# Spreading expert gates over the partitions by DMA instead of by a selection matmul, in an audio tower on one core

## Chip, cores and metric

One core of a Trainium2 chip. The metric is the device time of one execution in microseconds (us), lower is better. The kernel before was run three times, median 1820.26 us (1820.25 to 1823.58).

## What is computed

The reference is an audio tower of two layers over 4 sequences of 750 frames with 128 channels. Layer 0 is a dynamic convolution (31 taps), a dense convolution to 512 channels with SELU, a projection to 128 and a causal attention; its output has 720 positions per sequence, 2880 tokens in all. Layer 1 is an attention over 7200 keys per sequence and then a mixture of experts, which is what the change touches:

```python
router_probs = softmax(x @ router_w.T + bias)            # 64 experts
topk_p, topk_i = top_k(router_probs, 6); topk_p /= sum(topk_p) + 1e-9
# an assignment past the capacity C of its expert is dropped
hg = einsum('ecd,efd->ecf', expert_in, w_gate)           # F = 64
hu = einsum('ecd,efd->ecf', expert_in, w_up)
expert_out = einsum('ecf,edf->ecd', silu(hg) * hu, w_down)
out = x + shared_out + segment_sum(gate * expert_out)    # + 2 shared experts, halved
```

## The kernel before

The kernel (`tower`) has one instruction stream for each engine, and they wait for each other on semaphores. Stage 0 is layer 0, stage 1 the attention over the keys, stage 2 the experts. At the end of stage 1 all five engines meet at a barrier (`stage_end`).

**Router.** After the attention of sequence b its tokens go through the steps of `POST_STEPS`, which are laid by hand beside the tiles of the next sequence's attention (for the last sequence, beside the expert pairs of chunk 0, by the last number of each entry). The last steps are `gates`: VectorE multiplies probabilities and slots into `gate2` (L1219, twice, since the 64 experts stand in it twice), TensorE transposes it (L1512) to experts on 128 partitions, ScalarE writes the high halves as fp16 into `gates` and `g_tmp` (L804, L805), and VectorE writes the remainders into partitions 64 to 127 (L1226). So `gates` [128, 2880] holds the high fp16 part of a gate on partition e and the low part on partition 64 + e.

**Experts.** All experts are computed for all tokens. The tokens are cut into `NMC` = 6 chunks of `MT` = 480, and a chunk has `NSEQ` = 33 turns: turn 0 is the pair of shared experts, turns 1 to 32 (`PAIRS`) are pairs of routed experts, whose 2 x 64 hidden channels fill the 128 partitions. Inputs and weights are split in a high and a low fp16 part, so each product takes three matmuls. For turn n:

- TensorE, `up` (L1669): waits `up_free`, then 3 matmuls for the gate projection and 3 for the up projection (L1676 to L1678, once for each), and for a routed pair one more (L1682) with the 0/1 matrix `sel_sb`, which adds high and low part and spreads the two gates of the pair over 64 partitions each, into a third PSUM bank. That matmul signals `up_ps`.
- ScalarE, `silu` (L843): reads the gate projection.
- VectorE, `product` (L1278): L1282 multiplies silu (SBUF) with the up projection (PSUM) into `su`; L1288 multiplies `su` (SBUF) with the spread gates (PSUM) into `ac`, then `up_free` is raised. `shared_product` (L1296) has no gate.
- ScalarE, `high_part` (L849): fp16 copy `a_hi` of `ac`. In its order of work it stands behind the silu of turn n + 1.
- GpSimd, `low_part` (L643): `a_lo` = `ac` - `a_hi`, all three in SBUF.
- TensorE, `down` (L1686): 3 matmuls (L1690 to L1692) that add to the chunk's output.

Everything of a turn has two buffers. TensorE's order is up(n + 2), down(n), up(n + 3), down(n + 1), and so on. At the end of a chunk `chunk_done` copies the sum (L853), transposes it (L1699), adds the residual (L1305) and stores it from SyncE's queue (L538). Chunks 1 to 5 run in a hardware loop, chunk 0 is unrolled because of the router steps beside it. SyncE does nothing else in stage 2. In stage 1 it loads keys, values, `sel_sb` (L529) and the expert weights (L533).

Of the kernel before, what the change touches and what calls it, by code (L numbers as in the profile page):

```python
# [17 lines left out]
F32 = mybir.dt.float32  # L18
F16 = mybir.dt.float16
# [9 lines left out]
P = 120  # L29
# [89 lines left out]
def shared_turns():  # L119
# [4 lines left out]
    for b in range(B + 1):  # L124
        for x in steps + [(DOWN, B - 1, "h", k) for k in range(2)] * (b == B):
# [4 lines left out]
            if kind == MIX and at == 0:  # L130
# [30 lines left out]
              ("act", "gates", 0, 52, 26), ("dve", "gates", 1, 53, 27), ("pe", "gates", 1, 55, 28),  # L161
              ("act", "gates", 1, 56, 30), ("dve", "gates", 2, 56, 31)]
# [74 lines left out]
def tower(nc, d, out):  # L237
    ctx = ExitStack()
    with ctx:
# [54 lines left out]
        for n in range(2):  # L294
# [7 lines left out]
        sel_sb = region_k.take(PAIRS * 128, dtype=F16)  # L302
# [79 lines left out]
        gate2 = region_c.take(R, 2 * E)[0:P]  # L382
        g_tmp = region_c.take(T, dtype=F16)
# [13 lines left out]
        fin = region_c.take(MT // P, C)[0:P]  # L397

        band_dram = nc.dram_tensor("band_dram", [WT, NW, HEADS * WIN], F32).ap()
# [10 lines left out]
            shifted_logits logits_exp msk_ready gates_ready gates_hi  # L410
# [9 lines left out]
        s_tail = sem("tail_in")  # L420

# [59 lines left out]
        def _(sp):  # L481
# [47 lines left out]
            sp.dma_start(sel_sb, d["sel"]).then_inc(s["const_in"], 16)  # L529
# [6 lines left out]
            with sp.Fori(0, NMC) as c:  # L536
                sp.wait_ge(s["fin_ready"], c + 1)
                sp.dma_start(out_t[:, bass.ds(c * (MT // P), MT // P), :], fin).then_inc(s["fin_out"], 16)  # L538
# [119 lines left out]
        def _(act):  # L658
# [131 lines left out]
            def post(b, what, k):  # L790
# [11 lines left out]
                elif what == "gates":  # L802
                    act.wait_ge(s["post_full"], USE[POST, b, what, k])
                    a.activation(gates[0:E, b * T + k * HALF:b * T + (k + 1) * HALF], bank(bk, E)[:, 0:HALF], ACT.Copy)  # L804
                    a.activation(g_tmp[E:128, half], ps[E:128, bk, 0:HALF], ACT.Copy).then_inc(s["gates_hi"], 1)  # L805
# [72 lines left out]
        def _(dve):  # L878
# [263 lines left out]
            def post(b, what, k):  # L1142
# [74 lines left out]
                elif (what, k) == ("gates", 0):  # L1217
                    for n in range(2):
                        last = v.tensor_tensor(gate2[:, :, n * E:(n + 1) * E], slot[:, :, 0:E], probs[:, :, 0:E],  # L1219
                                               ALU.mult)  # L1220
                    own.link(last)
                    dve.sem_inc(s["gates_ready"], 1)
                elif what == "gates":
                    half = slice((k - 1) * HALF, k * HALF)
                    dve.wait_ge(s["gates_hi"], 2 * b + k)
                    own.link(v.tensor_tensor(gates[E:128, b * T + (k - 1) * HALF:b * T + k * HALF],  # L1226
# [99 lines left out]
        def _(pe):  # L1326
# [379 lines left out]
            for n in range(NSEQ):  # L1706
                if n + 2 < NSEQ:
                    up(0, n + 2, n + 1, n % 2, n + 2)
# [111 lines left out]
```

## Time and profile before

| | |
|---|---|
| median of three runs | 1820.26 us (1820.25 to 1823.58) |
| the profiled execution | 1822.85 us, its span 1821.1 us |
| busy: TensorE, its weight loads, VectorE, ScalarE, GpSimd | 90%, 60%, 62%, 39%, 25% of the span |
| granted TensorE clock, mean | 0.962 of full speed |
| stage 2 | from the barrier (first matmul at 1368.08 us) to the end |

The span is the time from the first to the last recorded instruction. Engines are PE (TensorE), PEld (its weight loads), DVE (VectorE), ACT (ScalarE), POOL (GpSimd) and SP (SyncE); a line of the profile gives busy time, a count and durations, and in brackets the idle time of the engine before the instruction and what ended it. Matmuls are pipelined: one that is shown with 0.37 us is followed 0.20 us later by the next.

### The profile page before, as it was taken

Reading aid. Unit: us, or ns where it says so; the run is one execution under the profiler, and the core shown is the slowest. Engines: PE = TensorE matmul, PEld = TensorE weight load, DVE = VectorE, ACT = ScalarE, POOL = GpSimd, SP = SyncE. Lnnn points to the kernel's source line nnn. Section 1 sums busy time; section 2 is a strip of 40 time slices with the busy share of each in tenths; the row PEclk is TensorE's granted clock in tenths of the full one; section 3 lists DMA queues with packets and bytes.
Section 4 is the critical chain, followed back from the end, with each engine's and each line's share of the span. In section 5 each row is a group of like instructions: output and inputs, shape, how many; then the busy total and the mean of one; then the engine's idle time right before and its main releaser. Section 6 shows DMA issues by size and latency. Waiting matters only on the chain.

```text
span 1821.1 us, 35248 instructions
## 1 busy us (share of the span) xinstructions
PE 1641.2 (90%) x12174; PEld 1097.0 (60%) x12174; DVE 1132.4 (62%) x2285; ACT 707.5 (39%) x1196; POOL 453.3 (25%) x443
## 2 busy tenths in 40 slices
PE   1689999999986789997999889989997899999998
PEld 1456766666654467776777667767783444444443
DVE  3763556554368776677666766676447666666665
ACT  1321121211101245544455344545564455555554
POOL 2110000000022221102110111107904345555554
PEclk7799999999998899999999899999999999999999
DMA  7320110100012211111111111111200000000000
GB/s 177 117 60 26 27 29 14 34 25 6 1 29 70 74 44 48 40 33 45 36 39 33 41 30 48 40 40 57 73 1 1 1 6 5 0 5 5 0 5 5
DMA packets 49509, 62.39 MB, mean 34 GB/s; under 512 B 18214, under 2 KB 30974, under 8 KB 48254
## 3 DMA queue, kind: packets, MB, share of 16 engines
q1 hardware_dynamic: 34269, 49.50, 9.6%
q0 software_dynamic: 1152, 8.39, 1.5%
q10 hardware_dynamic: 13984, 3.07, 1.1%
q8 instruction: 71, 1.16, 0.3%
q14 instruction: 33, 0.26, 0.0%
HBM read 56.40 MB, written 4.55 MB: 33 GB/s over the span
## 4 chain that ended last, share of the span: by engine, by line
PE 52%; DVE 21%; issue 16%; POOL 6%; DMA 2%; ACT 2%; POOLq 1%; DVEq 0%; SPq 0%; ACTq 0%
POOL region_c L643 5%; PE ps L1434 5%; PE ps L1436 5%; PE ps L1435 5%; PE ps L1588 4%; DVE region_c L1087 4%; DVE region_c L1080 3%; PE ps L1584 3%; PE ps L1585 3%; PE ps L1558 3%; PE ps L1567 3%; PE ps L1534 3%; PE ps L1562 3%; PE ps L1559 3%; PE ps L1522 3%
## 5 line engine op out<-in xcount | busy, mean ns | idle before, releaser
L1087 DVE TENSOR_REDUCE region_c<-ps 120x1 f32<-120x512 f32 (+1 forms) x336 | 225.8, 687 | 154.6 <-PE ps L1534 152.9
L763 ACT ACTIVATE region_c<-ps 128x720 f16<-128x720 f32 (+1 forms) x228 | 175.7, 771 | 297.1 <-PE ps L1567 297.1
L643 POOL TENSOR_TENSOR region_c<-region_c 128x480 f16<-128x480 f32 x198 | 218.7, 1105 | 268.9 <-ACT region_c L849 268.9
L1080 DVE TENSOR_TENSOR region_c<-ps,region_c 128x720 f16<-128x720 f32 (+1 forms) x228 | 205.7, 903 | 77.9 <-ACT ps L764 73.7
L1434 PE MATMUL ps<-region_k 128*128 128x360 f16 (+1 forms) x752 | 240.1, 319 | 6.0 <-ACT m L742 6.0
L1436 PE MATMUL ps<-region_k 128*128 128x360 f16 (+1 forms) x752 | 239.4, 318 | 0.0
L1435 PE MATMUL ps<-region_k 128*128 128x360 f16 (+1 forms) x752 | 239.1, 318 | 0.0
L1282 DVE SCALAR_TENSOR_TENSOR region_c<-region_c,ps 128x480 f32<-128x480 f32 x192 | 125.5, 654 | 119.7 <-PE ps L1682 113.1
L1584 PE MATMUL ps<-region_k,region_c 128*120 128x129 f16 (+2 forms) x1368 | 184.9, 223 | 0.0
L1585 PE MATMUL ps<-region_k,region_c 128*120 128x129 f16 (+2 forms) x1368 | 184.5, 223 | 0.0
L843 ACT ACTIVATE region_c<-ps 128x480 f32<-128x480 f32 x198 | 112.5, 571 | 168.9 <-PE ps L1678 167.8
L764 ACT ACTIVATE ps<-ps 128x720 f32<-128x720 f32 (+1 forms) x228 | 174.4, 765 | 0.0
L1585 PEld LDWEIGHTS ps<-region_k,region_c 128*120 128x120 f16 (+1 forms) x1368 | 164.8, 135 | 15.9 <-issue 1.6
L1584 PEld LDWEIGHTS ps<-region_k,region_c 128*120 128x120 f16 (+1 forms) x1368 | 169.0, 136 | 8.8 <-issue 0.9
L1676 PE MATMUL ps<-region_b,region_k 128*128 (+1 forms) x396 | 146.7, 371 | 13.3 <-DVEq L1290 10.6
L1588 PE MATMUL ps<-region_k,region_c 128*120 128x129 f16 (+2 forms) x1368 | 120.4, 225 | 37.2 <-DVE region_c L1080 36.1
L1558 PE MATMUL ps<-region_b,region_k 128*128 128x360 f16 (+1 forms) x456 | 145.7, 325 | 7.2 <-DVEq L1216 4.8
L1677 PE MATMUL ps<-region_b,region_k 128*128 (+1 forms) x396 | 146.2, 369 | 0.0
L1678 PE MATMUL ps<-region_b,region_k 128*128 (+1 forms) x396 | 146.1, 369 | 0.0
L1559 PE MATMUL ps<-region_b,region_k 128*128 128x360 f16 (+1 forms) x456 | 145.6, 324 | 0.0
L578 POOL TENSOR_TENSOR vare<-mv,eps 120x6 f32<-120x6 f32 x20 | 4.0, 199 | 566.7 <-DVE mv L997 566.7
L1534 PE MATMUL ps<-region_k,region_b 128*120 128x512 f16 (+1 forms) x336 | 130.8, 405 | 11.3 <-DVE region_c L1087 8.3
(229 smaller groups left out, 2898.3 us busy)
## 6 DMA issues: line engine op xcount, KB each, us to landing
region_c<-in_k SPq DMA_DIRECT2D x56, 256.0 KB, 2.9
region_c<-in_v SPq DMA_DIRECT2D x56, 256.0 KB, 2.7
region_c<-in_WcT POOLq DMA_DIRECT2D x8, 1024.0 KB, 8.0
region_c<-in_experts SPq DMA_DIRECT2D x18, 352.0 KB, 3.0
gates<-band_dram SPq DMA_DIRECT2D x28, 189.0 KB
region_c<-in_xw SPq DMA_DIRECT2D x28, 63.0 KB
region_c<-in_xT SPq DMA_DIRECT2D x4, 384.0 KB, 3.1
band_dram<-gates ACTq DMA_DIRECT2D x2, 756.0 KB, 11.1
```

The lines of the kernel that those rows point to most:

```text
L643: g.tensor_tensor(a_lo[u], ac[u], a_hi[u], ALU.subtract).then_inc(s["a_lo_ready"], 1)
L1080: v.tensor_tensor(halves(p_lo[u][0:parts]), two(2 * u, parts), halves(p_hi[u][0:parts]), ALU.subtract).then_inc(s["lo_ready"], 1)
L1087: v.tensor_reduce(mxk[:, r, bass.ds(c + 1, 1)], bank(bk, P), AX, ALU.max).then_inc(s["mx_free"], 1)
L1434: mm(o, wh[:, m, j], xh[:, j:j + w], start=(j == 0), stop=False)
L1435: mm(o, wh[:, m, j], xl[:, j:j + w], start=False, stop=False)
L1436: last = mm(o, wl[:, m, j], xh[:, j:j + w], start=False, stop=(j == n - 1))
L1534: mm(bank(bk, P), q_hi[:, b, r * P:(r + 1) * P], k_hi[b % 2][:, bass.ds(c2 * (2 * CH) + u * CH, CH)], start=True, stop=True).then_inc(s["m ...
L1558: mm(bank(2 * u + w, parts)[:, 0:HALF], kh, q_hi[:, b, q], start=True, stop=False)
L1559: mm(bank(2 * u + w, parts)[:, 0:HALF], kh, q_lo[:, b, q], start=False, stop=False)
L1584: mm(sums(r), ph, vh, start=False, stop=False, skip_group_check=True)
L1585: mm(sums(r), ph, vl, start=False, stop=False, skip_group_check=True)
L1588: last = mm(sums(r), p_lo[u][0:parts, r * P:(r + 1) * P], vh, start=False, stop=False, skip_group_check=True)
```

## The change

The gates are kept in fp32 on 64 partitions (`gate_t`), stored to device memory (`gates_dram` [64, 2880]) once for each sequence from ScalarE's queue, and read back by SyncE's queue: for each pair and chunk two DMAs, each of which writes one row of 480 gates (1920 bytes) into 64 partitions. They land in four buffers `gt`, three in the former place of `gates` and one in `region_k`, each used by every fourth pair. The second multiplication of `product` reads such a buffer in place of the PSUM bank. The selection matmul, the matrix `sel_sb` and its load, the second copy in `gate2`, the split into `g_tmp` and the two remainder steps of VectorE are gone. The loop over the pairs in VectorE's stream takes four pairs at a time, and the stores of finished chunks stand between the gate loads in SyncE's stream.

```diff
-              ("act", "gates", 0, 52, 26), ("dve", "gates", 1, 53, 27), ("pe", "gates", 1, 55, 28),
-              ("act", "gates", 1, 56, 30), ("dve", "gates", 2, 56, 31)]
+              ("act", "gates", 0, 52, 26), ("pe", "gates", 1, 55, 27), ("act", "gates", 1, 56, 28)]
...
-        sel_sb = region_k.take(PAIRS * 128, dtype=F16)
...
-        gate2 = region_c.take(R, 2 * E)[0:P]
-        g_tmp = region_c.take(T, dtype=F16)
+        gate2 = region_c.take(R, E)[0:P]
+        gate_t = region_c.take(T)[0:E]
...
+        region_k.at = KSET
+        gt = [gates32[:, n * MT:(n + 1) * MT] for n in range(3)] + [region_k.take(MT)]
+
+        gates_dram = nc.dram_tensor("gates_dram", [E, B * T], F32).ap()
...
-            sp.dma_start(sel_sb, d["sel"]).then_inc(s["const_in"], 16)
...
-            with sp.Fori(0, NMC) as c:
-                sp.wait_ge(s["fin_ready"], c + 1)
-                sp.dma_start(out_t[:, bass.ds(c * (MT // P), MT // P), :], fin).then_inc(s["fin_out"], 16)
+            def spread(c, p4, u):
...
+                for k in range(2):
...
+                    sp.dma_start(gt[u][64 * k:64 * k + 64, :], row.broadcast_to((64, MT))).then_inc(s_gt[u], 16)
+
+            sp.wait_ge(s["gates_out"], 16 * (B - 1))
+            for u in range(4):
+                spread(0, 0, u)
+            with sp.Fori(1, PAIRS // 4) as p4:
+                for u in range(4):
+                    sp.wait_ge(s["a_ready"], 4 * p4 + u - 2)
+                    spread(0, p4, u)
+            sp.wait_ge(s["gates_out"], 16 * B)
+            with sp.Fori(1, NMC) as c:
+                for p4 in range(PAIRS // 4):
+                    if p4 == 2:
+                        sp.wait_ge(s["fin_ready"], c)
+                        sp.dma_start(out_t[...], fin).then_inc(s["fin_out"], 16)
+                    for u in range(4):
+                        sp.wait_ge(s["a_ready"], NSEQ * c + 4 * p4 + u - 2)
+                        spread(c, p4, u)
...
-                    a.activation(gates[0:E, b * T + k * HALF:b * T + (k + 1) * HALF], bank(bk, E)[:, 0:HALF], ACT.Copy)
-                    a.activation(g_tmp[E:128, half], ps[E:128, bk, 0:HALF], ACT.Copy).then_inc(s["gates_hi"], 1)
+                    if b and k == 0:
+                        act.wait_ge(s["gates_out"], 16 * b)
+                    a.activation(gate_t[:, half], bank(bk, E)[:, 0:HALF], ACT.Copy).then_inc(s["gate_turned"], 1)
+                    act.wait_ge(s["gate_turned"], 2 * b + k + 1)
+                    act.sem_inc(s["post_free"], 1)
+                    if k == 1:
+                        act.dma_start(gates_dram[:, b * T:(b + 1) * T], gate_t).then_inc(s["gates_out"], 16)
...
-                    for n in range(2):
-                        last = v.tensor_tensor(gate2[:, :, n * E:(n + 1) * E], slot[:, :, 0:E], probs[:, :, 0:E],
-                                               ALU.mult)
-                    own.link(last)
+                    own.link(v.tensor_tensor(gate2, slot[:, :, 0:E], probs[:, :, 0:E], ALU.mult))
...
-                elif what == "gates":
-                    half = slice((k - 1) * HALF, k * HALF)
-                    dve.wait_ge(s["gates_hi"], 2 * b + k)
-                    own.link(v.tensor_tensor(gates[E:128, b * T + (k - 1) * HALF:b * T + k * HALF],
-                                             ps[E:128, bk, 0:HALF], g_tmp[E:128, half], ALU.subtract))
-                    dve.sem_inc(s["post_free"], 1)
...
-            def product(n, u, m):
+            def product(n, u, m, turn, k):
...
                 dve.wait_ge(s["down_done"], n + 1)
-                v.tensor_tensor(ac[u], su[u], bank(3 * u + 2)[:, 0:MT], ALU.mult).then_inc(s["a_ready"], 1)
+                dve.wait_ge(s_gt[k], 32 * turn + 32)
+                v.tensor_tensor(ac[u], su[u], gt[k], ALU.mult).then_inc(s["a_ready"], 1)
...
-                with dve.Fori(0, PAIRS // 2) as i:
-                    product(n0 + 2 * i + 1, 1, PAIRS * c + 2 * i + 1)
-                    product(n0 + 2 * i + 2, 0, PAIRS * c + 2 * i + 2)
+                with dve.Fori(0, PAIRS // 4) as i:
+                    for k in range(4):
+                        m = 4 * i + k + 1
+                        product(n0 + m, (k + 1) % 2, PAIRS * c + m, PAIRS // 4 * c + i, k)
...
-                    last = nc.tensor.transpose(bank(bk)[:, r * P:(r + 1) * P], gate2[:, 3 * k + r, :],
+                    last = nc.tensor.transpose(bank(bk, E)[:, r * P:(r + 1) * P], gate2[:, 3 * k + r, :],
...
-            def up(c, sq, pair, u, n):
+            def up(c, sq, u, n):
...
-                if pair is not None:
-                    last = mm(bank(3 * u + 2)[:, 0:MT], sel_sb[:, bass.ds(pair * 128, 128)], gates[:, at],
-                              start=True, stop=True)
                 last.then_inc(s["up_ps"], 1)
```

## Rows read from the trace of the kernel before

**Rows 1.** Page, part 1: busy us, share of the span, instructions of each engine.

```profile
PE 1641.2 (90%) x12174; PEld 1097.0 (60%) x12174; DVE 1132.4 (62%) x2285; ACT 707.5 (39%) x1196; POOL 453.3 (25%) x443
```

**Rows 2.** Windows view, two stretches: engines' busy time, granted clock, DMA share, GB/s.

```profile
1550.00:1600.00 50.00, 50.00 (x249) 23.70 (x247) 32.07 (x50) 26.55 (x50) 26.82 (x26) 1.00 0.00 0
1380.00:1385.00 5.00, 3.09 (x13) 1.02 (x13) 4.75 (x12) 1.17 (x2) 1.47 (x2) 1.00 0.01 3
```

**Rows 3.** Timeline, end of chunk 2: start us, duration us, engine, line.

```profile
1599.53 0.65 DVE L1282 SCALAR_TENSOR_TENSOR region_c<-region_c,ps 128x480 f32<-128x480 f32 x1 [0.68 <-PE ps L1682]
...
1599.86 0.37 PE L1676 MATMUL ps<-region_b,region_k 128*128 x1
...
1600.21 0.65 DVE L1288 TENSOR_TENSOR region_c<-region_c,ps 128x480 f32<-128x480 f32 x1
...
1600.67 0.57 ACT L843 ACTIVATE region_c<-ps 128x480 f32<-128x480 f32 x1 [0.96 <-PE ps L1678]
...
1601.08 0.37 PE L1682 MATMUL ps<-gates,region_k 128*128 x1
...
1601.14 0.59 ACT L849 ACTIVATE region_c<-region_c 128x480 f16<-128x480 f32 x1
...
1601.55 0.65 DVE L1282 SCALAR_TENSOR_TENSOR region_c<-region_c,ps 128x480 f32<-128x480 f32 x1 [0.68 <-PE ps L1682]
...
1601.81 1.10 POOL L643 TENSOR_TENSOR region_c<-region_c 128x480 f16<-128x480 f32 x1 [0.93 <-ACT region_c L849]
...
1602.96 0.38 PE L1690 MATMUL ps<-region_c,region_k 128*128 128x480 f16 x1 [0.91 <-POOL region_c L643]
```

**Rows 4.** Source view of two lines: duration ns min/median/max.

```profile
L1288 DVE TENSOR_TENSOR region_c<-region_c,ps x192: 653/653/655, 1373.2 to 1811.7; 128x480 f32<-128x480 f32 x192
...
L1206 DVE TENSOR_TENSOR region_c<-region_c x4: 559/560/1430, 987.7 to 1435.4; 120x384 f32<-120x384 f32 x4
```

**Rows 5.** Timeline, two places where VectorE and GpSimd instructions overlap.

```profile
1373.97 1.02 DVE L1148 TENSOR_TENSOR xres<-xres,rows 120x768 f32<-120x768 f32 x1 [0.15 <-DVE region_c L1288]
...
1374.54 1.42 POOL L643 TENSOR_TENSOR region_c<-region_c 128x480 f16<-128x480 f32 x1 [0.35 <-ACT region_c L849]
...
1435.34 1.10 POOL L643 TENSOR_TENSOR region_c<-region_c 128x480 f16<-128x480 f32 x1 [2.49 <-ACT region_c L849]
...
1435.42 1.43 DVE L1206 TENSOR_TENSOR region_c<-region_c 120x384 f32<-120x384 f32 x1
```

**Rows 6.** Timeline, chunk 0, a pair that VectorE paces.

```profile
1395.75 0.65 DVE L1288 TENSOR_TENSOR region_c<-region_c,ps 128x480 f32<-128x480 f32 x1
1396.43 0.60 ACT L849 ACTIVATE region_c<-region_c 128x480 f16<-128x480 f32 x1 [2.85 <-DVE region_c L1288]
...
1396.61 0.65 DVE L1282 SCALAR_TENSOR_TENSOR region_c<-region_c,ps 128x480 f32<-128x480 f32 x1 [0.21 <-DVE region_c L1288]
...
1397.11 1.10 POOL L643 TENSOR_TENSOR region_c<-region_c 128x480 f16<-128x480 f32 x1 [3.13 <-ACT region_c L849]
```

**Rows 7.** Timeline of VectorE, last product of chunk 2, first of chunk 3.

```profile
1602.24 0.65 DVE L1288 TENSOR_TENSOR region_c<-region_c,ps 128x480 f32<-128x480 f32 x1
...
1609.74 0.65 DVE L1288 TENSOR_TENSOR region_c<-region_c,ps 128x480 f32<-128x480 f32 x1
```

**Rows 8.** Timeline of VectorE, three gate products of chunk 0.

```profile
1412.01 0.65 DVE L1288 TENSOR_TENSOR region_c<-region_c,ps 128x480 f32<-128x480 f32 x1
...
1446.18 0.65 DVE L1288 TENSOR_TENSOR region_c<-region_c,ps 128x480 f32<-128x480 f32 x1
...
1462.66 0.66 DVE L1288 TENSOR_TENSOR region_c<-region_c,ps 128x480 f32<-128x480 f32 x1
```

**Rows 9.** DMA view, timeline of SyncE's queue, windows view at the kernel's start.

```profile
region_c<-in_k SPq DMA_DIRECT2D x56, 256.0 KB, 2.9
...
699.83 0.33 SPq L523 DMA_DIRECT2D region_c<-in_v  x1
...
30.00:40.00 10.00, 0.00 (x0) 0.00 (x0) 9.04 (x6) 4.71 (x5) 3.50 (x3) 0.50 0.86 78
```

More of the change, by code:

```diff
@@ L409, in tower @@
             st_ps p_hi_ready exp_sum lo_ready pv_done acc_ps acc_free wf_done
-            shifted_logits logits_exp msk_ready gates_ready gates_hi
+            shifted_logits logits_exp msk_ready gates_ready gate_turned gates_out
             gate_ps up_ps up_free silu_done a_ready a_hi_ready a_lo_ready down_done
@@ L420, in tower @@
         s_tail = sem("tail_in")
+        s_gt = [sem(f"gates_in{u}") for u in range(4)]
         def bank(n, parts=128):
@@ L535, in _ @@
             out_t = out.rearrange("b (r p) c -> p (b r) c", p=P)
-            with sp.Fori(0, NMC) as c:
-                sp.wait_ge(s["fin_ready"], c + 1)
-                sp.dma_start(out_t[:, bass.ds(c * (MT // P), MT // P), :], fin).then_inc(s["fin_out"], 16)
+            def spread(c, p4, u):
+                at = bass.ds(sp.snap(c * MT), MT) if not isinstance(c, int) else slice(c * MT, (c + 1) * MT)
+                for k in range(2):
+                    if isinstance(p4, int):
+                        row = gates_dram[8 * p4 + 2 * u + k:8 * p4 + 2 * u + k + 1, at]
+                    else:
+                        row = gates_dram[bass.ds(sp.snap(p4 * 8 + (2 * u + k)), 1), at]
+                    sp.dma_start(gt[u][64 * k:64 * k + 64, :], row.broadcast_to((64, MT))).then_inc(s_gt[u], 16)
[11 more added lines that the diff above has]
+                        sp.wait_ge(s["fin_ready"], c)
+                        sp.dma_start(out_t[:, bass.ds(sp.snap(c * (MT // P) - MT // P), MT // P), :], fin
+                                     ).then_inc(s["fin_out"], 16)
+                    for u in range(4):
+                        sp.wait_ge(s["a_ready"], NSEQ * c + 4 * p4 + u - 2)
+                        spread(c, p4, u)
+            sp.wait_ge(s["fin_ready"], NMC)
+            sp.dma_start(out_t[:, (NMC - 1) * (MT // P):, :], fin).then_inc(s["fin_out"], 16)
             sp.wait_ge(s["fin_out"], 16 * (NMC + 1))
@@ L1311, in _ @@
             for n in range(1, NSEQ):
-                product(n, n % 2, n)
+                product(n, n % 2, n, (n - 1) // 4, (n - 1) % 4)
                 for x in beside(B, "dve", pair=n):
@@ L1701, in chunk_done @@
                 last.then_inc(s["out_ps"], 1)
-            up(0, 0, None, 0, 0)
-            up(0, 1, 0, 1, 1)
+            up(0, 0, 0, 0)
+            up(0, 1, 1, 1)
             for n in range(NSEQ):
                 if n + 2 < NSEQ:
-                    up(0, n + 2, n + 1, n % 2, n + 2)
+                    up(0, n + 2, n % 2, n + 2)
                 if n + 1 < NSEQ:
@@ L1718, in _ @@
                 pe.wait_ge(s["up_free"], n0 + 2)
-                up(c, 0, None, 0, n0)
+                up(c, 0, 0, n0)
                 down(PAIRS, 0, n0 - 1, stop=True)
-                up(c, 1, 0, 1, n0 + 1)
+                up(c, 1, 1, n0 + 1)
                 chunk_done(c - 1)
-                up(c, 2, 1, 0, n0 + 2)
+                up(c, 2, 0, n0 + 2)
                 down(0, 0, n0, start=True)
                 with pe.Fori(0, PAIRS // 2 - 1) as i:
-                    up(c, 2 * i + 3, 2 * i + 2, 1, n0 + 2 * i + 3)
+                    up(c, 2 * i + 3, 1, n0 + 2 * i + 3)
                     down(2 * i + 1, 1, n0 + 2 * i + 1)
-                    up(c, 2 * i + 4, 2 * i + 3, 0, n0 + 2 * i + 4)
+                    up(c, 2 * i + 4, 0, n0 + 2 * i + 4)
                     down(2 * i + 2, 0, n0 + 2 * i + 2)
```

## Prediction, made before the changed kernel was run

> **What bounds the kernel now.** I read the page first: TensorE is busy for 90% of the span [rows 1], so an instruction taken from it looks like time. The change lies in stage 2, though, so next comes the windows view of a stretch inside it: TensorE has no idle time, at the full granted clock, 249 matmuls in 50 us [rows 2]. A turn has ten, so a pair takes 10 x 50 / 249 = 2.01 us. The timeline shows what each engine does in a pair [rows 3]: the two VectorE instructions of 0.65 us start 0.68 us apart, and VectorE then idles 0.68 us until the selection matmul L1682 is done. TensorE is the bound, but the chain behind it is long: ScalarE's L849 ends at 1601.73, GpSimd's L643 runs from 1601.81 to 1602.91, and the down matmul that needs it starts at 1602.96.
>
> **What the change takes from TensorE.** One matmul of ten, 0.20 us a pair, 192 of them. If nothing else ended last, a pair would take 1.81 us. It can't quite: down(n + 2) needs the silu of turn n + 3, whose up follows down(n). Along that loop [rows 3]: down 0.60 (three at 0.20), start of up to start of silu 0.81 (1599.86 to 1600.67), silu to L849 0.47, L849 0.59, to L643 0.08, L643 1.10, to the down matmul 0.05. Sum 3.70 us for two pairs, 1.85 a pair. So the most that this part gives is 0.16 us a pair.
>
> **What the change adds to VectorE.** L1288 read one operand from PSUM and now reads both from SBUF. In 192 executions beside GpSimd work it took 653 to 655 ns [rows 4]. An instruction with both inputs in SBUF does not stay at its own time: L1206 takes 560 ns, but 1430 in one execution [rows 4]. The timeline has the cause. GpSimd's L643 ran from 1435.34 to 1436.44, L1206 started 0.08 us after it and ended at 1436.85, 0.41 us behind L643's end. Alone it takes 0.56 for its 384 elements, start-up included, so it had passed none of them before L643 ended. The other way round, L1148 (two SBUF inputs) ran to 1374.99, and L643, started inside it, took 1.42 us instead of 1.10, ending 0.97 us behind it [rows 5]. Whichever starts first is left alone, the other waits.
>
> The Trainium skill (SBUF — State Buffer, Who interferes with whom) has this as a rule: a VectorE instruction with two SBUF inputs contends with a GpSimd instruction that reads SBUF, and the later one is blocked until the first ends. Rows 5 agree. Without the rule and rows 5 the sum would be the 1.85 us a pair above; with it, it is the one below.
>
> Who starts first in the changed kernel? Take E as the end of L1288 of turn n. Where VectorE sets the pace [rows 6], E is 1396.40: L849 starts 0.03 later, L643 0.71 later, and it ends 1.81 after E. VectorE's next L1282 starts 0.21 after E, and L1288 follows 0.69 later, at E + 0.90. So L643 of turn n is always under way when L1288 of turn n + 1 comes, by 0.19 us. L1288 waits until E + 1.81 and then needs 0.41 x 480 / 384 = 0.51 us. It ends at E + 2.32, which is the next E. **A pair takes 2.32 us**, L1288 is shown with 1.42 us, and TensorE waits about 0.5 us a pair. The pattern starts by itself: at the pace of now, too, L1288 of the next turn comes inside the running L643 (1602.24, between 1601.81 and 1602.91 [rows 3, 7]), and is untouched only because it reads PSUM.
>
> **Chunks 1 to 5.** A chunk has 31 gaps from product to product: 31 x (2.32 - 2.01) = +9.6 us. The passage from the last product of a chunk to the first of the next takes 7.50 us [rows 7]; it is a chain of latencies in which one selection matmul (0.20) lies and the down matmuls start about 0.1 earlier, and L1288 meets no L643 there: -0.3. Together +9.3 a chunk, **+46.5 us**.
>
> **Chunk 0** has the router steps beside it. Where a step of over about 0.9 us stands between two products, L1288 comes after L643's end and nothing is added. Two stretches are quick: 8 gaps from 1395.75 to 1412.01, 16.26 us, become 8 x 2.32 = 18.6; and 8 gaps from 1446.18 to 1462.66, 16.48 us, also 18.6 [rows 6, 8]. That is +4.4; I leave one more short gap against the dropped second L1219. **+4.5 us**.
>
> **What is hidden.** The dropped L1226, L1219, L805 of sequences 0 to 2 lie beside the attention, where TensorE is hardly idle: 0 (at most 3 x 1.6 = 5 us saved). The load of `sel_sb`: SyncE then waits for the barrier for tens of us, 0. ScalarE's store of the gates and its issue: 0.33 us for an issue [rows 9] on an engine that is busy 1.2 of 2.3 us: 0; for the last sequence it has four pairs and a chunk end to land.
>
> **The gate loads.** They queue on SyncE behind nothing but each other and one store a chunk. An issue takes 0.33 us, a 256 KB load lands 2.9 us after it [rows 9]; two DMAs of 120 KB make 0.7 + 2.9 = 3.6 us. A buffer is asked for when L1288 of a pair ends and is needed three pairs and 0.90 us later: 3 x 2.32 + 0.90 = 7.9 us. Hidden, with 4 us to spare. No row shows one DRAM row sent to 64 partitions in this size. Bounds: 0, and, from the worst rate in the trace (78 GB/s at 0.86 of the DMA engines' time, short writes [rows 9]), 0.246 MB in 3.15 us a pair, so +1.1 us over today's pair and 177 us in all. I take 0: these are runs of 1920 bytes, like the key loads. At the start of stage 2 the first pair could wait 1 to 2 us once.
>
> **Sum.** 46.5 + 4.5 = +51. The profiled execution took 1822.85 us (span 1821.1) and would take 1873.9; it lies 2.6 over the median, on which the forecast stands: 1820.3 + 51 = **1871 us**. Its own range is 1850 to 1886 (2.2 to 2.4 us a pair, and up to 5 us saved in stage 1).
>
> **Rivals.**
> 1. *L1288 keeps its 0.65 us.* For it: it kept it beside L643 in all executions so far, and rows 5 are of other lines. Against: what differs is the PSUM operand, which the change removes. Then 155 gaps at 1.85 instead of 2.01 give -24, passages -1.5, chunk 0's 16 quick gaps -3: **1792 us, faster**. It decides from the point where a pair comes under 2.01 us, that is, with L1288 shown at under 1.42 - 0.31 = 1.11 us.
> 2. *GpSimd is the one that waits*, L1288 getting in first: From the end of L1288 of turn n + 1: L643 of turn n ends 0.97 behind it, its down starts 0.05 later and takes 0.60, up(n + 3) ends and L1282 starts 1.47 after that (five matmuls of 0.20, the last with 0.37, and 0.10), and L1288 ends 1.33 later [rows 3]. Sum 4.42 for two pairs, 2.21 a pair: 1820 + 155 x 0.20 + 2 = **1853 us**. Against: the 0.19 us of lead [rows 6].
> 3. *The gate loads are late*: **over 1900, up to 1997 us**. Against: the 4 us to spare.
> 4. *The clock falls* because TensorE now idles a fifth of the time. In chunk 0 it had 13 matmuls in 5 us, half of what it can do, at a granted clock of 1.00 [rows 2]. At the lower level a pair's nine matmuls take 3.6 us; a tenth of the time there adds 160 x 0.13 = 21: **1891 us**.
>
> **Chances.** Forecast 0.73, rival 1 0.10, rival 2 0.05, rival 3 0.07, rival 4 0.05. About 0.2% (3.6 us) is what a measurement of this kernel can tell from no change; some of rivals 1 and 2 could land within it if blocking is partial, 0.02. Faster 0.09, same 0.02, slower 0.89. The range 1845 to 1895 takes in the forecast's, rival 2 and a mild rival 4.
>
> **What would show it.** In the changed profile: L1288's successor with a median near 1.4 us while L643 stays at 1.10; idle TensorE of about 0.5 us a pair ended by a semaphore of VectorE or by L643; 9 x 50 / 2.32 = 194 matmuls in 50 us of stage 2; VectorE's busy time up by some 0.77 x 171 = 130 us (155 gaps and 16 in chunk 0); `gt` loads landing in about 3 us with no wait on them. L1288's successor at 0.65 us, or a wait for the DMA ahead of it, would prove the forecast wrong.

## The result and the profile after

The changed kernel takes **1871.25 us**, the median of four runs (1868.13 to 1876.55), against 1820.26 us before (1819.81 to 1823.58, four runs): a ratio of 1.028, 95% interval 1.0257 to 1.0303, slower. In a second comparison (`e8` below) it was 1.0288 (1.0259 to 1.0318). The forecast was 1871 us, its range 1845 to 1895. The profiled execution took 1872.18 us, its span 1870.2 us.

Part 1 of the page after (busy us, share of the span, instructions), beside [rows 1]:

```profile
PE 1646.1 (88%) x11982; PEld 1060.0 (57%) x11982; DVE 1219.9 (65%) x2273; ACT 720.6 (39%) x1188; POOL 452.1 (24%) x443
```

192 matmuls are gone and TensorE is as busy as before; VectorE runs twelve instructions less and is busy 87.5 us longer. The source view of the gate multiply (now L1315) and of GpSimd's low part (L672) says which of them grew, beside [rows 4] (duration ns min/median/max; under "who waited" us in total and times):

```profile
L1315 DVE TENSOR_TENSOR region_c<-region_c,gates x144: 657/1270/1524, 1369.3 to 1858.4; 128x480 f32<-128x480 f32 x144
L1315 DVE TENSOR_TENSOR region_c<-region_c,region_k x48: 657/1270/1418, 1382.6 to 1860.7; 128x480 f32<-128x480 f32 x48
...
who waited for it (us, times):
  ACT region_c L884: 145.9, 187
  DVE region_c L1308: 70.7, 169
```

```profile
L672 POOL TENSOR_TENSOR region_c<-region_c x198: 1091/1095/1349, 1369.2 to 1862.7; 128x480 f16<-128x480 f32 x198
```

The multiply went from 653 ns to a median of 1270, and GpSimd's instruction (L672, L643 before) stayed at its 1.10 us: VectorE is the one that waits. The timeline of the changed kernel in chunk 3 (start us, duration us, engine, line) shows how, beside [rows 3] and [rows 6]:

```profile
1631.09 0.65 DVE L1308 SCALAR_TENSOR_TENSOR region_c<-region_c,ps 128x480 f32<-128x480 f32 x1 [0.36 <-DVE region_c L1315]
...
1631.44 1.09 POOL L672 TENSOR_TENSOR region_c<-region_c 128x480 f16<-128x480 f32 x1 [1.94 <-ACT region_c L884]
...
1631.78 1.27 DVE L1315 TENSOR_TENSOR region_c<-region_c,gates 128x480 f32<-128x480 f32 x1
...
1632.70 0.37 PE L1715 MATMUL ps<-region_c,region_k 128*128 128x480 f16 x1 [0.38 <-POOL region_c L672]
...
1633.08 0.60 ACT L884 ACTIVATE region_c<-region_c 128x480 f16<-128x480 f32 x1 [0.76 <-DVE region_c L1315]
...
1633.41 0.66 DVE L1308 SCALAR_TENSOR_TENSOR region_c<-region_c,ps 128x480 f32<-128x480 f32 x1 [0.36 <-DVE region_c L1315]
...
1633.76 1.09 POOL L672 TENSOR_TENSOR region_c<-region_c 128x480 f16<-128x480 f32 x1 [1.23 <-ACT region_c L884]
...
1634.10 1.27 DVE L1315 TENSOR_TENSOR region_c<-region_c,gates 128x480 f32<-128x480 f32 x1
```

L672 runs from 1631.44 to 1632.53. The gate multiply starts inside it, at 1631.78, and ends at 1633.05, 0.52 us behind it. 2.32 us later the same three stand there again (1633.41, 1633.76, 1634.10). TensorE's `down` starts 0.17 us after L672's end and had waited. The multiply is shown with 1.27 and not the forecast 1.42 because L1308 starts 0.36 us after the last multiply instead of 0.21, so it comes 0.15 us later into the same wait; in every fourth pair (the turn of the loop) the gap is 0.69 and the multiply is shown with 0.77. The pair stays at 2.32, since only the end counts.

In the windows view, beside [rows 2], TensorE's 249 matmuls in 50 us are now 192 (194 were forecast), still at the full clock. In chunk 0 the clock was below it in places:

```profile
1550.00:1600.00 50.00, 44.15 (x192) 15.71 (x192) 38.82 (x44) 24.67 (x43) 23.00 (x21) 1.00 0.36 110
...
1375.00:1380.00 5.00, 3.45 (x11) 1.07 (x12) 4.62 (x12) 1.78 (x3) 1.85 (x3) 0.72 0.14 51
1380.00:1385.00 5.00, 4.76 (x14) 1.49 (x12) 4.75 (x8) 1.69 (x3) 2.23 (x2) 0.60 0.24 57
...
1395.00:1400.00 5.00, 5.00 (x21) 2.45 (x20) 3.81 (x5) 2.38 (x5) 2.02 (x3) 0.73 0.37 111
...
1415.00:1420.00 5.00, 5.00 (x18) 2.10 (x17) 2.66 (x7) 2.05 (x4) 1.09 (x1) 0.68 0.08 26
```

The kernel before has one such place in its chunk 0:

```profile
1415.00:1420.00 5.00, 5.00 (x16) 2.38 (x15) 1.90 (x5) 1.06 (x2) 1.09 (x1) 0.51 0.01 2
1420.00:1425.00 5.00, 5.00 (x21) 2.22 (x20) 2.43 (x4) 3.36 (x5) 1.10 (x1) 0.80 0.00 0
```

Leaving out the first 3 us of stage 2, which both kernels begin at the lower level, the granted clock is at the lower level for 13.6 us of chunk 0 after and for 6.8 us before.

The gate loads, beside [rows 9] (KB each, us to landing), are as quick to land as the key loads (an issue takes 0.47 us and not the forecast's 0.33), and no wait of L1315 for a DMA stands among the waits:

```profile
gates<-gates_dram SPq DMA_DIRECT2D x288, 120.0 KB, 2.7
...
region_k<-gates_dram SPq DMA_DIRECT2D x96, 120.0 KB, 2.8
```

By stage, in one profiled execution each (us; a chunk is measured from copy to copy of the chunk sums, the passage from the end of its last gate multiply to the end of the next one's first):

| | before | after | forecast | difference |
|---|---|---|---|---|
| stage 2 starts at | 1368.1 | 1364.2 | 0 (at most -5) | -3.9 |
| chunk 0, up to the copy of its sum | 97.9 | 102.4 | +4.5 | +4.5 |
| each of chunks 1 to 5 | 69.88 | 79.60 | +9.3 | +9.72 |
| of it a passage | 7.50 | 7.60 | -0.3 | +0.10 |
| of it 31 gaps, each | 2.01 | 2.32 | +0.31 | +0.31 |

-3.9 + 4.5 + 5 x 9.72 = +49.2, and the spans of these two executions differ by 49.1; the medians differ by 51.0.

### The profile page after: what moved, and what is told of

The parts are those of the page before. It is cut to its first block, busy times and chain, and to the rows that moved or that the text cites. A ratio compares the mean times of both kernels' runs of the same rounds, so it can differ in the third digit from the quotient of the medians.

```text
span 1870.2 us, 35973 instructions
## 1 busy us (share of the span) xinstructions
PE 1646.1 (88%) x11982; PEld 1060.0 (57%) x11982; DVE 1219.9 (65%) x2273; ACT 720.6 (39%) x1188; POOL 452.1 (24%) x443
## 4 chain that ended last, share of the span: by engine, by line
PE 49%; DVE 21%; issue 18%; POOL 6%; DMA 2%; ACT 2%; POOLq 1%; DVEq 1%; SPq 0%; ACTq 0%
POOL region_c L672 5%; PE ps L1462 5%; PE ps L1464 5%; PE ps L1463 5%; PE ps L1616 4%; DVE region_c L1122 3%; DVE region_c L1115 3%; PE ps L1612 3%; PE ps L1613 3%; PE ps L1586 3%; PE ps L1562 3%; PE ps L1595 3%; PE ps L1590 3%; PE ps L1587 3%; PE ps L1550 3%
## 5 line engine op out<-in xcount | busy, mean ns | idle before, releaser
L672 POOL TENSOR_TENSOR region_c<-region_c 128x480 f16<-128x480 f32 x198 | 217.9, 1100 | 323.0 <-ACT region_c L884 323.0
L884 ACT ACTIVATE region_c<-region_c 128x480 f16<-128x480 f32 x198 | 119.3, 602 | 148.3 <-DVE region_c L1315 145.9
L1308 DVE SCALAR_TENSOR_TENSOR region_c<-region_c,ps 128x480 f32<-128x480 f32 x192 | 125.6, 654 | 77.4 <-DVE region_c L1315 70.7
L1315 DVE TENSOR_TENSOR region_c<-region_c,gates 128x480 f32<-128x480 f32 x144 | 159.0, 1104 | 12.3 <-DVE region_c L1308 8.6
```

What stands on the lines that cost most here:

```text
L672: g.tensor_tensor(a_lo[u], ac[u], a_hi[u], ALU.subtract).then_inc(s["a_lo_ready"], 1)
```

## The experiments

Eleven runs were made; e8 is the changed kernel once more. "Chunk" is one of chunks 1 to 5; "multiply" is the gate multiply's median (of its commoner form); the ratio is to the kernel before in the same comparison, whose medians there were 1815.7 (e1, e2, e3, e6), 1817.4 (e4, e5, e7, e8) and 1817.5 us (e9 to e11).

| | time us (runs) | ratio, 95% interval | chunk us | multiply ns |
|---|---|---|---|---|
| before (profiled) | 1820.26 | | 69.88 | 653 |
| after (profiled) | 1871.25 (4) | 1.028 (1.0257 to 1.0303) | 79.60 | 1270 |
| e1 before, operand in SBUF | 1878.08 (1) | | 79.46 | 990 |
| e2 before, no selection matmul | 1813.13 (10) | 0.9982 (0.9966 to 0.9998) | 69.10 | 653 |
| e3 after, su in PSUM | 1811.17 (10) | 0.9968 (0.9953 to 0.9983) | 69.42 | 657 |
| e4 after, GpSimd only writes | 1781.05 (1) | | 63.84 | 659 |
| e5 after, low part in two halves | 1837.90 (1) | | 75.66 | 861 |
| e6 after, no further gate loads | 1861.90 (4) | 1.0244 (1.0212 to 1.0277) | 79.42 | 1270 |
| e7 e3 with half a low part | 1781.34 (4) | 0.9809 (0.9789 to 0.9830) | 64.06 | 657 |
| e8 after again | 1867.44 (4) | 1.0288 (1.0259 to 1.0318) | 79.74 | 1270 |
| e9 e3, low part used last | 1785.64 (4) | 0.9827 (0.9795 to 0.9859) | 65.38 | 657 |
| e10 before, low part used last | 1815.13 (10) | 0.9991 (0.9971 to 1.0010) | 69.36 | 653 |
| e11 after, low part used last | 1866.36 (1) | | 79.62 | 1270 |

**e1: only the operand moves.** The kernel before keeps its selection matmul and loads nothing; its gate multiply reads a constant SBUF tile (filled once, ahead of stage 2).

```diff
+            own.link(v.memset(fixed, 0.25))
...
-                v.tensor_tensor(ac[u], su[u], bank(3 * u + 2)[:, 0:MT], ALU.mult).then_inc(s["a_ready"], 1)
+                v.tensor_tensor(ac[u], su[u], fixed, ALU.mult).then_inc(s["a_ready"], 1)
```

> The kernel before with one edit: the second multiplication of a pair reads a constant SBUF tile instead of the PSUM bank that the selection matmul still fills, so the gates have no effect on the output. Ten matmuls a pair stay, there are no gate loads. Theory (the two SBUF inputs collide with GpSimd's subtraction): the multiplication is shown with about 1.4 us, a pair takes 2.32 us instead of 2.01, and the time is 1820 + 46 + 4 = about 1870 us. Rival (the loads from device memory, or TensorE's gaps, are what costs in the changed kernel): the multiplication keeps 0.65 us, a pair 2.01 us, the time 1820 us.

Measured: 1878.08 us, 79.46 us a chunk. The timeline of e1:

```profile
1616.41 1.10 POOL L645 TENSOR_TENSOR region_c<-region_c 128x480 f16<-128x480 f32 x1 [1.23 <-ACT region_c L851]
...
1617.04 0.98 DVE L1291 TENSOR_TENSOR region_c<-region_c,region_k 128x480 f32<-128x480 f32 x1
...
1618.73 1.10 POOL L645 TENSOR_TENSOR region_c<-region_c 128x480 f16<-128x480 f32 x1 [1.23 <-ACT region_c L851]
...
1619.01 1.34 DVE L1291 TENSOR_TENSOR region_c<-region_c,region_k 128x480 f32<-128x480 f32 x1
```

The multiply starts 0.63 and 0.28 us into GpSimd's instruction, is shown with 0.98 and 1.34 us, and ends 0.51 and 0.52 us behind it. So the place of one operand alone gives the whole loss in the chunks, with TensorE's ten matmuls and no loads. That the time is 7 to 11 us above the changed kernel's does not come from the chunks: stage 2 of e1 begins at 1370.1 us, at the late end of what these runs show (see the last point on the prediction), and chunk 0 takes 103.3 us.

**e2: only the selection matmul goes.** It runs in the first turns alone; later turns multiply with what it left in the PSUM bank.

```diff
-                if pair is not None:
+                if pair is not None and isinstance(n, int) and n < 3:
```

> The kernel before with the selection matmul run only for the first two pairs; the multiplication goes on reading the two PSUM banks that these filled, so all pairs get the gates of pair 0 or 1. No SBUF operand, no gate loads. Theory: TensorE's loop of down, up, silu, high part, low part sets 1.85 us a pair, 155 gaps save 0.16 us each, chunk 0 and the chunk ends 3 to 5 us more, so about 1791 us. Rival (TensorE alone sets the pace, 1.81 us a pair): about 1784 us. If ScalarE or VectorE were the next bound: over 1805 us.

Measured: 1813.13 us, 0.2% faster than before: about a tenth of what was expected. Two pairs still take 4.01 us, as the timeline of e2 shows:

```profile
1628.87 0.65 DVE L1288 TENSOR_TENSOR region_c<-region_c,ps 128x480 f32<-128x480 f32 x1
...
1629.91 0.37 PE L1690 MATMUL ps<-region_c,region_k 128*128 128x480 f16 x1
...
1630.32 0.37 PE L1692 MATMUL ps<-region_c,region_k 128*128 128x480 f16 x1
...
1630.70 0.37 PE L1676 MATMUL ps<-region_b,region_k 128*128 x1
...
1631.52 0.57 ACT L843 ACTIVATE region_c<-ps 128x480 f32<-128x480 f32 x1 [1.13 <-DVEq L1290]
...
1631.98 0.60 ACT L849 ACTIVATE region_c<-region_c 128x480 f16<-128x480 f32 x1
...
1632.66 1.10 POOL L643 TENSOR_TENSOR region_c<-region_c 128x480 f16<-128x480 f32 x1 [1.09 <-ACT region_c L849]
...
1633.92 0.37 PE L1690 MATMUL ps<-region_c,region_k 128*128 128x480 f16 x1
```

It is the loop of the prediction, but with 0.38 us instead of 0.20 between `down`'s last matmul and `up`'s first (1630.32 to 1630.70), and `down` 0.16 us behind the low part instead of 0.05: 3.70 + 0.18 + 0.11 = 3.99 us.
```profile
L1725 PEldq ALU_OP  x1: 32/32/32, 1630.1 to 1630.1; - x1
L1725 PEldq COMPARE_BRANCH  x1: 208/208/208, 1630.2 to 1630.2; - x1
L1725 PEldq FUSED_REGOPS  x1: 110/110/110, 1630.4 to 1630.4; - x1
```

L1725 is the head of TensorE's loop over the pairs, two to a turn. The `up` at 1630.70 is the first of a new turn. The semaphore that it asks for is not what it waits for: the multiply that raises it ran from 1628.87 and ended 1.2 us earlier. Over chunks 1 to 5 the step from `down`'s last matmul to the next `up` at a turn of the loop has a median of 0.38 us in e2 and e3 (70 turns each); where no turn lies between, it is 0.20. In the kernel before the same three instructions stand at each turn, but they begin 0.1 us ahead of `down`'s first matmul (L1725 at 1597.1, L1690 at 1597.23), and the step is 0.20 at all 70 turns. In e2 the wait for L643 has held the instruction stream up, and they begin 0.2 us behind that matmul (1630.1, 1629.91). (The row of the silu names VectorE's L1290 as its releaser. The matmul that it needs, the third of `up`, started at 1631.11 and is shown until 1631.48, so that link of the loop is as the forecast had it.)

The 0.16 us (0.17 in the unrounded times) stand at a wait that a register instruction carries, ahead of the weight load (source view of e2, 1629.5 to 1630.5, first fence). The 0.05 of the forecast were read at the last `down` but one of a chunk, which stands behind the loop and has no such instruction, though TensorE had been idle for 0.91 us there too (source view of before, 1602.8 to 1603.0, second fence):

```profile
L1690 PEldq FUSED_REGOPS  x1: 74/74/74, 1629.8 to 1629.8; - x1
L1690 PEld LDWEIGHTS ps<-region_c,region_k x1: 95/95/95, 1629.9 to 1629.9; 128*128 x1
```

```profile
L1690 PEld LDWEIGHTS ps<-region_c,region_k x1: 95/95/95, 1603.0 to 1603.0; 128*128 128x128 f16 x1
```

So both terms belong to TensorE's own instruction stream in the loop. No run took either of them away; this is read from the traces.

**e3: the change, but its product of silu and up stays in PSUM.** The gate multiply then reads one operand from PSUM and the gates from SBUF. Nothing is left out; the third PSUM bank is free since the selection matmul is gone.

```diff
-                v.scalar_tensor_tensor(out=su[u], in0=sg[u], scalar=A_SCALE / X_SCALE ** 2,
+                v.scalar_tensor_tensor(out=bank(3 * u + 2)[:, 0:MT], in0=sg[u], scalar=A_SCALE / X_SCALE ** 2,
...
-                v.tensor_tensor(ac[u], su[u], gt[k], ALU.mult).then_inc(s["a_ready"], 1)
+                v.tensor_tensor(ac[u], bank(3 * u + 2)[:, 0:MT], gt[k], ALU.mult).then_inc(s["a_ready"], 1)
```

> The changed kernel with one edit: the product of silu and up projection is written into the PSUM bank that the selection matmul left free, so the multiplication by the gates reads one operand from PSUM and one from SBUF. All gate loads stay and the output is complete. Theory: no collision, the multiplication is back at 0.65 us, a pair takes 1.85 us, and the time is about 1788 us (1791 less the 3 to 4 us that stage 1 saved). Rival (the loads cost): it stays near 1871 us, or lands between, with waits for a DMA ahead of the multiplication.

Measured: 1811.17 us; the source view of its gate multiply has no execution above 659 ns, beside the same low part and the same loads:

```profile
L1315 DVE TENSOR_TENSOR region_c<-ps,gates x144: 656/657/659, 1362.8 to 1796.5; 128x480 f32<-128x480 f32 x144
```

All of the loss is gone, although 179 of the 192 multiplies start while a low part is running. The gain expected on top is missing as in e2: 69.42 us a chunk, held by the loop of 4.01 us.

**e4: GpSimd writes but does not read.** The changed kernel, its SBUF operands kept.

```diff
-                g.tensor_tensor(a_lo[u], ac[u], a_hi[u], ALU.subtract).then_inc(s["a_lo_ready"], 1)
+                g.tensor_tensor(a_lo[u][:, 0:2], ac[u][:, 0:2], a_hi[u][:, 0:2], ALU.subtract)
+                g.memset(a_lo[u][:, 2:MT], 0.0).then_inc(s["a_lo_ready"], 1)
```

> The changed kernel with GpSimd's low part replaced: it subtracts two columns and fills the other 478 with a constant, so GpSimd writes SBUF but reads hardly any of it. The low part of the result is thereby left out. Theory (VectorE with two SBUF inputs is held only by a GpSimd instruction that reads SBUF): the gate multiply L1315 falls from a median of 1.27 us back to about 0.66, and chunks 1 to 5 fall from 79.6 us each to 70 or less (65 to 70, less if the fill is quicker than the 1.10 us of the subtraction, which shortens the loop through it). Time 1790 to 1820. Rival (any GpSimd instruction on SBUF holds VectorE, or two SBUF inputs are slow by themselves): the multiply stays at 1.1 to 1.4 us, unless the fill takes much under 1.10 us; the fill's length and the multiply's start inside or outside it tell.

Measured: 1781.05 us, 63.84 us a chunk. Its timeline:

```profile
1612.89 0.50 POOL L673 MEMSET region_c<- 128x478 f16 x1
...
1613.10 0.66 DVE L1316 TENSOR_TENSOR region_c<-region_c,region_k 128x480 f32<-128x480 f32 x1
```

The fill runs until 1613.39; the multiply, begun inside it, takes its 0.66 us. 138 of the 192 multiplies start inside a fill, and none takes over 660 ns. Two SBUF inputs are not slow in themselves, and this GpSimd instruction, which only writes SBUF, does not hold them. The chunk is shorter than the 65 to 70 us expected, because the two GpSimd instructions together last 0.63 us in place of 1.10 and the loop falls with them.

**e5: the low part in two halves.**

```diff
-                g.tensor_tensor(a_lo[u], ac[u], a_hi[u], ALU.subtract).then_inc(s["a_lo_ready"], 1)
+                for q in range(2):
+                    at = slice(q * MT // 2, (q + 1) * MT // 2)
+                    last = g.tensor_tensor(a_lo[u][:, at], ac[u][:, at], a_hi[u][:, at], ALU.subtract)
+                last.then_inc(s["a_lo_ready"], 1)
```

> The changed kernel with GpSimd's low part as two subtractions of 240 columns. Theory (whichever starts first holds the other until it ends, instruction by instruction): the multiply L1315 comes at about 0.2 us after the first half began, waits for the end of that half alone, then runs for about 0.5 us, while the second half is held behind it. A half alone takes about 0.64 us; the low part then ends later by the multiply's 0.5, but the next product starts earlier: L1315 shown with 0.8 to 1.0 us, a pair 1.95 to 2.15 us, chunks of 69 to 75 us, time 1820 to 1850. Rival (the blocked engine is not let in between two instructions of the other): the multiply waits for both halves, 1.28 us and more, a pair of 2.4 to 2.5 us, chunks of over 80 us, time 1890 to 1910.

Measured: 1837.9 us, 75.66 us a chunk, as the theory had it but for 0.7 us a chunk. Its timeline, where two halves stand in one row:

```profile
1613.99 1.65 POOL L674 TENSOR_TENSOR region_c<-region_c 128x240 f16<-128x240 f32 x2 [1.27 <-ACT region_c L887]
...
1614.29 0.86 DVE L1318 TENSOR_TENSOR region_c<-region_c,region_k 128x480 f32<-128x480 f32 x1
```

A half alone takes 0.64 us, so the first ended at 1614.63; the multiply ended at 1615.15, 0.52 behind it, and the second half at 1615.64, 0.49 behind the multiply. The two engines take turns, instruction by instruction. Against e8, the changed kernel in the same comparison, that is 30 us less (1837.9 from one run against 1867.44); the spans of the two profiles differ by 26.0 us, of which 5 x 4.08 = 20.4 lie in chunks 1 to 5 and 4.2 in chunk 0. It stays slower than e3, where the two don't meet.

**e6 and e8: are the loads hidden?** e8 is the changed kernel as it is; e6 loads the gates of the first four pairs only and reuses them.

```diff
-            with sp.Fori(1, PAIRS // 4) as p4:
-                for u in range(4):
-                    sp.wait_ge(s["a_ready"], 4 * p4 + u - 2)
-                    spread(0, p4, u)
...
-                    for u in range(4):
-                        sp.wait_ge(s["a_ready"], NSEQ * c + 4 * p4 + u - 2)
-                        spread(c, p4, u)
...
-                dve.wait_ge(s_gt[k], 32 * turn + 32)
+                dve.wait_ge(s_gt[k], 32)
```

> The changed kernel with the gate loads issued for the first four pairs of chunk 0 alone; all other pairs use what these brought, so their gates are wrong. Both operands stay in SBUF. Theory: the loads are hidden, so nothing changes: 1871 us, within 3 us, the multiplication still 1.27 us at the median. Rival (the loads are late, or their writes to SBUF slow the multiplication): 1790 to 1850 us.

> The changed kernel as it is, for comparison with the others. Theory and rivals alike: ratio 1.028 to the kernel before, chunks of 79.5 to 79.7 us. What it asks is where stage 2 starts: 1364 us as in the first profile, against 1356 with the later gate loads taken away. If that stretch differs by up to 8 us here too, the loads have no part in it.

Measured: 1861.90 against 1867.44 us, intervals of the ratio 1.0212 to 1.0277 and 1.0259 to 1.0318, which overlap. e6 lies 6 us below the 1868 to 1874 that were expected of it, and its multiply is as expected. Stage 2 starts at 1356.1 and 1355.8 us, chunk 0 takes 100.7 and 101.9, a chunk 79.42 and 79.74. In stage 2 the profiles differ by 1.2 + 5 x 0.32 = 2.8 us, which is the most that 376 loads can be charged with. The 8 us by which stage 2 of e6 began earlier than in the first profile of after was there in e8 too, with all its loads.

**e7: what holds e2 and e3 at 2.0 us a pair?** e3 with a low part of 240 columns from the third pair on.

```diff
-                g.tensor_tensor(a_lo[u], ac[u], a_hi[u], ALU.subtract).then_inc(s["a_lo_ready"], 1)
+                at = slice(0, MT if isinstance(n, int) and n < 2 else MT // 2)
+                g.tensor_tensor(a_lo[u][:, at], ac[u][:, at], a_hi[u][:, at], ALU.subtract).then_inc(s["a_lo_ready"], 1)
```

> The kernel of e3_su_in_psum (the change, with the product of silu and up kept in PSUM) with GpSimd's low part over 240 of 480 columns, half of the low part of the result left out from the third pair on. It asks what holds a pair at 2.0 us there and with the selection matmul gone, when nine matmuls need 1.8. Theory (the loop of down, up, silu, L884, L672 and down again takes 4.01 us for two pairs, 1.10 of it L672): with about 0.64 for L672 the loop falls to 3.55, under TensorE's 2 x 1.80; a pair takes 1.80 to 1.87 us, chunks 1 to 5 take 63 to 66 us instead of 69.4, time 1780 to 1790. Rival (TensorE cannot be fed faster, or VectorE and ScalarE with their waits set 2.0): chunks stay within 1 us of 69.4, time 1805 to 1815.

Measured: 1781.34 us, 64.06 us a chunk, 1.83 us from multiply to multiply. L673 (the low part) takes 0.64 us and nothing else differs: the loop through it was what held the pair.

**e9, e10, e11: the loop shortened with nothing left out.** `down` first uses the high part twice, waiting for it alone, and the low part last; in e3, in the kernel before and in the changed kernel.

```diff
-                pe.wait_ge(s["a_lo_ready"], n + 1)
+                pe.wait_ge(s["a_hi_ready"], n + 1)
                 o = bank(6)[:, 0:MT]
                 mm(o, wd_hi[:, bass.ds(sq * C, C)], a_hi[u], start=start, stop=False)
-                mm(o, wd_hi[:, bass.ds(sq * C, C)], a_lo[u], start=False, stop=False)
-                mm(o, wd_lo[:, bass.ds(sq * C, C)], a_hi[u], start=False, stop=stop
+                mm(o, wd_lo[:, bass.ds(sq * C, C)], a_hi[u], start=False, stop=False)
+                pe.wait_ge(s["a_lo_ready"], n + 1)
+                mm(o, wd_hi[:, bass.ds(sq * C, C)], a_lo[u], start=False, stop=stop
                    ).then_inc(s["down_done"], 1)
```

> The kernel of e3_su_in_psum (the change, with the product of silu and up kept in PSUM) with down's matmuls in another order: the two that need only L884's high part come first and wait for it alone, the one that needs GpSimd's low part comes last. Nothing is left out. Theory (the loop of 4.01 us for two pairs through L672 sets a pair there): L672 may now end two matmuls (0.40 us) later against TensorE, the loop falls to 3.61 us, about TensorE's own 2 x 1.80. A pair takes 1.82 to 1.88 us, chunks 1 to 5 take 64 to 66 us instead of 69.4, time 1778 to 1792. Rival (the extra wait between the matmuls costs TensorE its 0.17 us gap each pair): 1.95 to 2.0 us a pair, chunks of 67.5 to 69.5, time 1800 to 1812.

> The kernel before with the same new order of down's matmuls. With ten matmuls a pair TensorE alone needs 2.0 us, so a shorter loop is worth nothing in the pairs, at most 0.4 us in each passage from chunk to chunk: chunks of 69.4 to 69.9 us, ratio 0.997 to 1.000. Rival (the loop and not TensorE's ten matmuls held the kernel before): chunks of 65 to 67 us, time about 1795. With e9 it says what the selection matmul costs once nothing else holds the pair: about 0.15 to 0.2 us a pair.

> The changed kernel with the same new order of down's matmuls, its product still in SBUF. Theory (the pace is set by VectorE's gate multiply waiting for GpSimd's L672, TensorE waits for both): a pair stays at 2.32 us, L1315 at a median of 1.27 us, chunks at 79 to 79.7 us, time 1862 to 1872. Rival (TensorE's loop through L672 is what makes the pair longer): chunks fall by 0.2 to 0.4 us a pair, to 67 to 74 us.

Measured: e9 1785.64 us and 65.38 us a chunk; e10 1815.13 and 69.36; e11 1866.36 and 79.62. All three went as the theory had it. In the timeline of e9 the low part of a turn ends when `down`'s first matmul (L1715) has just begun; its last (L1718) is the one that needs it:

```profile
1626.54 1.10 POOL L672 TENSOR_TENSOR region_c<-region_c 128x480 f16<-128x480 f32 x1 [0.78 <-ACT region_c L884]
...
1627.43 0.37 PE L1706 MATMUL ps<-region_b,region_k 128*128 x1
...
1627.63 0.37 PE L1715 MATMUL ps<-region_c,region_k 128*128 128x480 f16 x1
...
1627.83 0.37 PE L1716 MATMUL ps<-region_c,region_k 128*128 128x480 f16 x1
...
1628.03 0.37 PE L1718 MATMUL ps<-region_c,region_k 128*128 128x480 f16 x1
...
1628.33 0.37 PE L1704 MATMUL ps<-region_b,region_k 128*128 x1
```

L672 ends at 1627.64, and TensorE goes from `up` through `down` in steps of 0.20 us. Ahead of the next `up` (1628.03 to 1628.33) it still stands for 0.10 us, at the turn of its loop; that is once in two pairs, 0.05 of the 0.06 us by which the 31 gaps, at 1.86 us each, are longer than nine steps of 0.20. e10 shows that the same order is worth nothing in the kernel before, whose 31 gaps take 2.00 us each, ten matmuls of 0.20; e11 that it is worth nothing while VectorE waits for GpSimd. Three kernels with one edit, and in each another thing ends last. **e9 is the fastest kernel of the study that leaves nothing out**: 1.7% faster than before, and by the two ratios 0.9827 / 1.0288, some 4.5% faster than the change as made. With the order the same, the change with its product in PSUM (e9) against the selection matmul (e10) is worth 69.36 - 65.38 = 4.0 us a chunk.

## Why the prediction was right, point by point

- **"What the change adds to VectorE"**: right. The mechanism is shown by e1 (operand alone), e3 (operand back in PSUM), e4 (GpSimd's reads taken away) and e5 (instruction by instruction). The rule of the Trainium skill (SBUF — State Buffer, Who interferes with whom) that a VectorE instruction with two SBUF inputs contends with a GpSimd instruction that reads SBUF, and not with one that only writes it, is borne out by the traces in both halves: 1270 ns beside L672, 659 beside the fill of e4. The 0.51 us that the multiply needs after L672's end were 0.51 to 0.52. Rival 1 fell with this and so did rival 2, for L672 stayed at 1.09 to 1.10 in the steady pairs. VectorE's busy time grew by 87.5 us, not 130: the forecast had taken 1.42 us for every multiply, but in the loop VectorE comes to the multiply 0.15 us later, and 0.65 us later in every fourth pair, so that much less of the wait is shown, without moving the end.
- **"Chunks 1 to 5"**: +9.72 each instead of +9.3: right, and 0.4 us a chunk short. The gaps are 2.32 us as worked out; the passage, for which -0.3 was put down, came to +0.1. Without the selection matmul and with the operand in PSUM (e2) it is 7.57 us from start to start, against 7.50 before: the lost matmul is worth nothing there either.
- **"What the change takes from TensorE"**: wrong as a price, without weight for the sum. "The most that this part gives is 0.16 us a pair" was added up from rows of a kernel in which TensorE was never early in the pairs. Two terms were too small: `down` to `up`, put down with `down`'s 0.60 us alone, has 0.18 us more at each turn of TensorE's loop, and L643 to `down`, put down with 0.05, is 0.16 in the loop; the 0.05 were read at a `down` outside it. The loop is 4.01 and not 3.70 us for two pairs, and the part gives nothing: a steady pair of e2 takes 4.01 / 2 = 2.00 us. Rival 1's 1792 us would have been some 1813, as e2 and e3 show. Had VectorE kept its 0.65 us, the change as such would have been worth 0.2 to 0.3%.
- **"Chunk 0"**: +4.5 as forecast, but the agreement proves less than in the loop: past the first 3 us the granted clock was at its lower level for 13.6 us, against 6.8 before, so some of the 4.5 may be rival 4's. In e8, also with 13.6 us of it, chunk 0 took 101.9 us, and in e6, with none, 100.7: so the lower clock and the loads together come to about 1.2 us there. The parts were not separated further. In chunks 1 to 5 rival 4 has no part: 1.00 throughout the windows read.
- **"What is hidden"**: right for the loads (landing 2.7 to 2.8 us, no wait, at most 2.8 us by e6 and e8), so rival 3 fell. For stage 1, taken as 0 with at most 5 us saved, stage 2 began at 1360.2 to 1370.1 us in four profiles of kernels with the router steps of before (before, e1, e2, e10) and at 1354.8 to 1365.9 in nine with those of the change. That hints at several us saved; no run took those steps alone, so it stays open.
- **The sum**: that 1871 came out to the microsecond is in part luck. The profiled pair of executions has 2.1 us more in chunks 1 to 5 than forecast and 3.9 us less ahead of stage 2, where 0 was put down; and stage 2 of the changed kernel alone began 8 us apart in two profiles. What the runs bear out is the 2.32 us a pair, not the last digit of the sum.

## What to carry to other kernels

Before an operand is moved from PSUM to SBUF, look at what it leaves on the instruction that reads it: here a VectorE multiply whose two inputs both lie in SBUF takes turns with a GpSimd subtraction that reads SBUF, and if the two overlap in each pass of a loop, that makes a serial chain of two engines that the dependences do not ask for. Keeping one intermediate in PSUM, where a bank was free, undid it (e3). And the price of work taken from the busiest engine is only known when the next loop behind it has been added up with what that engine's own instruction stream costs once a wait holds it up: the turn of its loop, and the register instruction at a wait. A latency is to be read at the place in the loop where it will count. Here the loop behind took 4.01 us for two pairs where TensorE had taken 4.02, and only a second edit (the late operand used last) turned the freed time into a gain.

## What was not expected of the hardware

- At the turn of TensorE's hardware loop the step from one matmul to the next is 0.38 us and not 0.20 (medians of 70 turns in each of e2 and e3) once the stream has been held up at the `down` ahead of it; the three instructions of L1725 last 0.35 us together. In the kernel before, where nothing holds it up, it is 0.20 at all 70 turns.
- A matmul behind a wait starts 0.17 us after the end of the releasing instruction where a register instruction carries the wait (the 75 waits of this kind in e2 that held TensorE), and 0.06 us after it where the weight load itself does (30 in e2); TensorE had been idle in both. With the loop's turn this makes 0.29 us in two pairs and took back nearly all of the 0.32 us that the forecast saw to be had for two pairs (e2).
- An instruction of GpSimd that is held behind one of VectorE recovers like the reverse: 0.49 us for 240 columns after the multiply's end, of 0.64 alone (e5).
- The granted clock fell in chunk 0 after stretches of very different load: it was at the lower of its two levels (1.2 and 2.4 GHz) for most of 1375 to 1385 us in the changed kernel (0.72 and 0.60), after 12 matmuls in the 5 us ahead, and for nearly all of 1415 to 1420 us in the kernel before (0.51), after 29 matmuls in the 5 us ahead with TensorE busy throughout. In chunks 1 to 5 of the changed kernel, where TensorE idles between the pairs all the time, it stayed at 1.00. What makes it fall stays open.
